# Recommendation tower, one core: three 128-sample embedding tiles in a ring, four products taken one chunk ahead, and a new order of the pass

## What is computed

```python
e = jnp.stack([tbl_0[ids[:, 0]], ..., tbl_25[ids[:, 25]]], axis=1)   # 2048 x 26 x 128
sd = jnp.einsum('bfd,bd->bf', e, dense)
ss = jnp.einsum('bfd,bgd->bfg', e, e)
pairs = ss[:, iu, ju]                                                 # i < j
h = jnp.concatenate([dense, sd, pairs, dense], axis=1)
h = jnp.maximum(h @ W_top1 + b_top1, 0.0)                             # 512
h = jnp.maximum(h @ W_top2 + b_top2, 0.0)                             # 256
y = h @ W_top3                                                        # 1
```

## Time and profile before

| | us |
|---|---|
| median of 3 runs (401.68 to 403.55) | 402.63 |
| the profiled execution | 404.94 |
| its span, first to last instruction | 403.1 |
| PE busy | 337.3 (84%) |
| POOL busy | 277.5 (69%) |
| DVE busy | 234.1 (58%) |
| ACT busy | 204.8 (51%) |
| mean granted TensorE clock | 0.949 |

### The profile page before, as it was taken

One profiled execution on the slowest core, in us unless ns is written; L12 is line 12 of the kernel. 1 busy time (PEld: TensorE's weight loads), 2 busy tenths in 40 slices (PEclk: granted clock), 3 DMA queues, 4 the chain that ended last, 5 costly groups with the idle time before them and its releaser, 6 DMA issues.

```text
span 403.1 us, 14210 instructions
## 1 busy us (share of the span) xinstructions
PE 337.3 (84%) x6216; PEld 301.7 (75%) x6216; DVE 234.1 (58%) x702; ACT 204.8 (51%) x289; POOL 277.5 (69%) x295
## 2 busy tenths in 40 slices
PE   0556889898989889897989899896998989898585
PEld 0545679797878769795979779683987979796384
DVE  0969968682776438680867457670587538640321
ACT  2372545566466534666465553754346654565132
POOL 6777777777777777777777777777777777773000
PEclk9998989999999989999998999998899999899559
DMA  6998233222323214223323325122141323111000
GB/s 166 246 260 261 77 84 96 79 76 83 98 81 78 76 54 110 68 80 81 96 80 79 81 57 121 55 81 78 55 122 54 99 62 81 55 52 36 3 2 1
DMA packets 19118, 35.33 MB, mean 88 GB/s; under 512 B 7168, under 2 KB 8712, under 8 KB 19056
## 3 DMA queue, kind: packets, MB, share of 16 engines
q0 software_dynamic: 9216, 18.89, 17.8%
q1 hardware_dynamic: 9824, 15.52, 13.9%
q10 hardware_dynamic: 16, 0.01, 0.0%
HBM read 34.39 MB, written 0.01 MB: 85 GB/s over the span
## 4 chain that ended last, share of the span: by engine, by line
PE 55%; POOL 12%; ACT 11%; DMA 9%; issue 8%; DVE 3%; SPq 1%; POOLq 0%
PE et_ps L565 23%; POOL rows L290 12%; PE m_ps L525 10%; PE g_ps L486 8%; ACT et L371 8%; PE m_ps L536 6%; PE et_ps L555 5%; DMA et<-tbl_in 5%; DMA rows<-tbl_in,idx 3%; ACT zt_hi L346 2%; PE m_ps L545 2%; DMA idb<-ids_one_hot 1%; DVE one_hot L406 1%; DVE zt_lo L449 1%; DVE z L442 1%
## 5 line engine op out<-in xcount | busy, mean ns | idle before, releaser
L290 POOL DMA_INDIRECT rows<-tbl_in,idx x288 | 276.7, 961 | 89.3 <-issue 84.8
L406 DVE TENSOR_SCALAR one_hot<-idb,first_row 125x256 fp32r<-125x256 int32 x512 | 159.6, 384 | 81.5 <-PE et_ps L565 78.5
L371 ACT COPY et<-et_ps 128x384 f32<-128x384 f32 (+1 forms) x128 | 123.4, 1031 | 97.8 <-PE et_ps L565 76.7
L565 PE MATMUL et_ps<-one_hot,table_hi 125*128 125x256 f32 x512 | 132.7, 297 | 22.2 <-DVE one_hot L406 18.8
L565 PE MATMUL et_ps<-one_hot,table_lo 125*128 125x256 f32 x512 | 127.1, 286 | 0.0
L565 PEld LDWEIGHTS et_ps<-one_hot,table_hi 125*128 125x128 f32 x512 | 100.1, 195 | 29.2 <-issue 20.4
L565 PEld LDWEIGHTS et_ps<-one_hot,table_lo 125*128 125x128 f32 x512 | 100.0, 195 | 0.0
L555 PE MATMUL et_ps<-ident,rows 128*128 128x128 f32 x288 | 51.1, 291 | 16.6 <-DMA rows<-tbl_in,idx 11.9
L486 PE MATMUL g_ps<-et 128*27 128x26 f32 x4096 | 54.0, 193 | 11.4 <-issue 9.2
L486 PEld LDWEIGHTS g_ps<-et 128*27 128x27 f32 x4096 | 45.3, 106 | 23.0 <-issue 15.9
L555 PEld LDWEIGHTS et_ps<-ident,rows 128*128 128x128 f32 x288 | 32.6, 145 | 22.3 <-issue 13.1
(11 more groups left out here) (46 smaller groups left out, 284.5 us busy)
## 6 DMA issues: line engine op xcount, KB each, us to landing
idb<-ids_one_hot SPq DMA_DIRECT2D x32, 256.0 KB
rows<-tbl_in,idx POOLq DMA_INDIRECT x288
et<-tbl_in SPq DMA_DIRECT2D x7, 448.0 KB
xt<-dense_t SPq DMA_DIRECT2D x8, 128.0 KB, 3.9
z<-w_z SPq DMA_DIRECT2D x2, 256.0 KB, 5.9
et<-w SPq DMA_DIRECT2D x1, 512.0 KB, 6.9
gram<-tbl_in SPq DMA_DIRECT2D x1, 448.0 KB
et<-tbl_in SPq DMA_DIRECT2D x7, 52.0 KB
```

What stands on the lines that cost most here:

```text
L290: nc.gpsimd.indirect_dma_start(out=rows[:, r, n, :], out_offset=None, in_=tables[GATHERED[k]], in_offset=bass.IndirectOffsetOnAxis(idx[par ...
L371: nc.scalar.copy(dst, src).then_inc(et_copied, 1)
L406: last = nc.vector.tensor_scalar(one_hot[n % 2][0:KP, k, :], idb[0:KP, n // 2 % ID_RING, n % 2, :], first_row[0:KP, 0:1], float(k), ALU.su ...
L565: last = nc.tensor.matmul(ps[:, n % 2 * CH:n % 2 * CH + CH], part[0:KP, n, k, :], one_hot[n % 2][0:KP, k, :], start=k == 0 and part is tab ...
```

## The change

- `et` becomes one ring of three tiles of 128 samples (two a chunk) where there were two of 256.
- O0 to O3 of chunk c+1 are done at the end of the pass in which the rest of chunk c is looked up; `PLAN` lists all steps of the kernel with their chunk. What waits for what is worked out from the place in this list.
- The one-hot rows are a ring of 16 rows (two units); each row is announced and given back by itself, where a whole unit was. B steps are gone: unit n+1 is built at step O n.
- The order of a pass is another (`PHASE`). G steps come in twos. In passes without a next chunk the steps of that chunk are left out.
- An O pair is copied to `et` in two instructions of 256 columns, one per tile, and the dense features in two of 128.
- At the start the tables go through four places (three in the third tile of `et`, one in `gram`). The dense features and three blocks of the first layer's weights are loaded behind the fourth table. The gather indices are loaded at once for all chunks (the first chunk's 36 columns first).
- As before: eight one-hot tables, 18 gathered ones, a ring of eight slots of rows, 288 gathers, and the same matmuls.

```diff
-SCHEDULE = [(step[0], int(step[1:])) for step in (
-    "O0 B2 G4 O1 B3 G5 T0 G6 O2 B4 G7 O3 B5 A0 T1 A1 O4 O5 A2 T2 A3 T3 Z0 Z1 T4 T5 Z2 B6 B7 L0 T6 L1 T7 "
-    "O6 O7 T8 L2 G0 T9 G1 G2 T10 G3 T11 L3").split()]
+PHASE = [(step[0], int(step[1:])) for step in (
+    "T0 G4 G5 O4 T1 O5 G6 G7 T2 A0 A1 T3 O6 A2 A3 O7 Z0 T4 Z1 T5 Z2 "
+    "T6 G0 G1 L0 T7 G2 G3 T8 L1 O0 T9 O1 L2 T10 O2 T11 L3 O3").split()]
+def later(kind, n):
+    if kind == "O" and n < AHEAD:
+        return 1
+    return -1 if kind in "AZL" or kind == "G" and n >= G_STEPS // 2 else 0
+AHEAD = 4
+OH_RING = 16
+STAGES = 4
+PLAN = [(kind, p + later(kind, n), n) for p in range(-1, NCH + 1) for kind, n in PHASE
+        if 0 <= p + later(kind, n) < NCH]
...
-        one_hot = [sb(f"one_hot{i}", [128, KT, CH], f32r) for i in range(2)]
+        one_hot = sb("one_hot", [128, OH_RING, CH], f32r)
-        et = [sb(f"et{i}", [128, CH * FW]) for i in range(2)]
+        et = sb("et", [128, ET_TILES * TILE_W])
...
+            for n, f in enumerate(ONE_HOT):
+                if n >= STAGES:
+                    sp.wait_ge(table_lo_done, n - STAGES + 1)
+                if n == 6:
+                    load_ids(2)
...
+                if n == 1:
+                    sp.dma_start(idx[:, first:], ids_gather[:, first:]).then_inc(idx_in[1], 16)
+                    load_ids(1)
+                if n == STAGES - 1:
+                    load_dense(0)
+                    load_dense(1)
+                    for k in range(KZ):
...
+                if kind == "O" and n % 2 == 1:
+                    act.wait_ge(oh_used, (c * NO + n + 1) * KT)
+                    src = et_ps[SLOT["O", c, n - 1] % 2][:, :].rearrange("d (f t b) -> d t f b", f=2, t=TILES)
+                    for t in range(TILES):
+                        last = nc.scalar.copy(et_fields(TILES * c + t, NG + n - 1, 2), src[:, t])
+                    last.then_inc(et_copied, 1)
+                if kind == "O" and c == 0 and n + STAGES < NO:
+                    table_hi_part(n + STAGES)
...
+            def build(unit):
+                pair, half = divmod(unit, 2)
+                if half == 0:
+                    dve.wait_ge(idb_in[pair % ID_RING], (pair // ID_RING + 1) * 16)
+                for k in range(KT):
+                    at = unit * KT + k
+                    wait(dve, oh_used, at - OH_RING + 1)
+                    nc.vector.tensor_scalar(one_hot[0:KP, at % OH_RING, :], idb[0:KP, pair % ID_RING, half, :],
+                                            first_row[0:KP, 0:1], float(k), ALU.subtract, ALU.is_equal)\
+                        .then_inc(oh_ready, 1)
+                if unit + 1 < NO:
+                    table_lo_part(unit + 1)
...
+                if kind == "G" and c == 0 and n == G_STEPS // 2 - 1:
+                    split_weights()
...
+                    for k in range(KT):
+                        at = (c * NO + n) * KT + k
+                        pe.wait_ge(oh_ready, at + 1)
...
+                        last.then_inc(oh_used, 1)
```

556 lines of the change are left out of this document (253 added, 303 removed).

## The result

| | before | after |
|---|---|---|
| median (lowest to highest of 4 runs each) | 403.09 (401.68 to 404.51) | 422.64 (418.79 to 424.97) |
| profiled execution; its span | 404.94; 403.1 | 420.60; 418.8 |
| last gather starts | 366.57 | 380.28 |
| from there to the end of the span | 36.5 | 38.5 |

The account below looks back on a forecast made before the run. GpSimd's unhindered chain of 288 gathers was taken to bound the kernel: 3.33 + 363.24 + (36.53 + 0.3) + 1.84 = 405.2 us profiled, 402.9 beside the median of 402.63; range 399.8 to 406.8.

Parts of the forecast that it names:

- The pass: One TensorE pass over a chunk: claimed to keep its pace of about 43 us, covered by the gathers, price 0.
- The walk: Step-by-step sum of TensorE's work through one pass, ending at 41.8 us; with hand-overs 43, bounds 41.5 and 46.
- About 1 us for hand-overs: Allowance in a TensorE pass for hand-overs between engines, added to the walk to reach 43 us.
- The 43.2 of before: TensorE's pass in the kernel before, measured between 79.92 and 123.08, when held by its own work and its partners.
- The start: Loading of tables and first gathers: claimed TensorE frees row slots about 1.1 us early, cost nothing, bounds 0 and +4.
- Rival 2: GpSimd is held up in the start by late tables; at 4 us late, 405.9 us; chance 0.14.
- Rival 3: TensorE's pass exceeds 45.2 us, so it falls behind its rows; at 46 us a pass, 408.8 us; chance 0.12.
- the lag: How far T0 of the second chunk runs behind its rows: claimed 8 us, as before, worked off by the last T11.
- 8.7 us for the missing steps: Last pass, T0 to T11: time off a full pass, for three O fewer and L3 and O3 standing behind T11.
- The point of 45.2: TensorE pass length in us up to which gathers cover it; from there on the cover is gone.
- The end: After the last gather: terms 0.8 + 1.0 - 1.5 sum to +0.3 us, bounds -3.3 and +1.8.
- term (d): End of kernel: TensorE's 0.32 and 2.73 us issue gaps in the last products shrink; -1.5 us, bounds 0 and -3.05.

Follow-up runs that it names:

- order of before, new rings: Changed kernel keeping its rings, row-wise hand-over, copies per tile and load start, but with the kernel before's whole order, builds included, and no products ahead: 404.43 us.
- own builds: Combined kernel with O7's unit built right behind O6's, the next chunk's first two behind Z2, and A0, O6, A1, T3, A2, O7, A3, T4 in sequence: 405.53 us.
- old steps, builds at O: Changed kernel with the kernel before's order of steps and no products ahead, but VectorE still building unit n+1 at step O n: 427.31 us.
- T0 late: Changed kernel with G4 and G5 moved ahead of T0 in the pass: 420.2 us, ratio 1.0396.
- spacer: Changed kernel with one small VectorE instruction, adding an SBUF column to itself, behind each packing of z: 424.99 us, ratio 1.0528.
- indices early: Changed kernel with the fourth pair of indices loaded ahead of SyncE's waits for the last weights: 421.24 us, ratio 1.0465.
- builds alone: Changed kernel with only VectorE's builds moved: O7's unit right behind O6's, the next chunk's first two behind the split of Z2: 410.06 us, ratio 1.0106.
- combined: Changed kernel with three edits: O6 ahead of A0 and next chunk's first build behind Z2; G4, G5 ahead of T0; fourth index pair early: 410.11 us.
- builds away from packing: Changed kernel with O6 ahead of A0 on all engines and the next chunk's first unit built behind the split of Z2: 424.71 us, ratio 1.0559.
- by units of eight: Changed kernel with one-hot rows handed over by whole units of eight again, ring and order kept: 444.26 us, ratio 1.0925.
- one gather of three: Both kernels with only the first of three tables in a slot gathered: changed kernel 410.8 us, kernel before 389.05 and 395.15 us.

## Where the prediction went wrong, step by step

**The frame held.** The time is the later of GpSimd's chain with a tail of about 36 us and TensorE's own chain. The kernels above, by that rule:

| kernel | last gather | tail | held gathers | set by |
|---|---|---|---|---|
| before | 366.57 | 36.5 | 0 | gathers |
| order of before, new rings | 367.50 | 36.1 | 0 | gathers |
| own builds | 368.39 | 36.4 | 0 | gathers |
| old steps, builds at O | 392.89 | 36.0 | 7, of 4.5 to 5.0 us | gathers |
| T0 late | 381.87 | 36.1 | 9 | gathers |
| spacer | 387.50 | 35.1 | 12 | gathers |
| changed | 380.28 | 38.5 | 8 | TensorE, by 2 to 3 us |
| indices early | 380.18 | 38.1 | 6 | TensorE, by 2 us |
| builds alone | 366.46 | 41.3 | 0 | TensorE |
| combined | 367.12 | 42.8 | 0 | TensorE |
| builds away from packing | 367.86 | 52.5 | 0 | TensorE |
| by units of eight | 393.10 | 53.2 | 9 | TensorE |

**The pass was the step that failed.** The walk gave 41.8 us and 1 us of hand-overs; T0 to T0 took 46.4 in the pass from 211.33 to 257.74. Its pieces, each against the walk: T0's wait for the copy of O2/O3 was missing (+1.3). The G pairs were taken at 1.5 to 1.6 from runs of 64 that followed one another; they take 1.8 to 2.1 (four pairs, +1.3). The first layer's L0, at 3.8 us instead of 2.9, ran its first matmuls slowly (0.41 us each, not 0.28) behind the waits of Z:

```profile
230.46 0.43 PE L482 MATMUL a_ps<-ident,z 64*128 64x64 f32 x4 [1.11 <-issue]
230.82 0.55 PE L435 MATMUL et_ps<-ident,rows 128*128 128x128 f32 x3
231.29 2.04 PE L462 MATMUL g_ps<-et 128*27 128x26 f32 x128
...
233.64 0.41 PE L498 MATMUL m_ps<-x_hi,w_lo 128*128 128x256 f32 x1
```

Two windows of this L0 (columns as for the passes; the granted clock is the third figure from the end) show the lower of the two levels, 1.2 GHz, and then the higher:

```profile
233.20:234.80 1.60, 1.60 (x12) 1.55 (x9) 0.00 (x0) 0.88 (x1) 1.29 (x2) 0.50 0.32 79
235.20:236.80 1.60, 1.60 (x16) 1.60 (x15) 0.00 (x0) 0.00 (x0) 1.14 (x2) 1.00 0.14 41
```

I had put the lower clock into the end of the kernel only, not into the pass (+0.9 here; in the pass from 175.91 on, at 1.00, L0 takes 3.06). O1, at 3.4 instead of 3.0, started behind a build that had itself waited for the split of L1 (+0.4). The other pieces add 0.7. The walk had seen the waits for builds and packing, each within about 0.6 us. What it lacked was T0's wait for the copy, the price of the G products and the clock behind a wait. "About 1 us for hand-overs", which had to hold all that the walk left out, was the mis-sized term; it was 4.6.

**The same error hid the width.** The bounds of 41.5 and 46 came from the walk, and the measured mean of 46.9 lies above them. The 43.2 of before was taken as a check of the walk, though it holds the hand-overs of another order, and is one pass at full clock.

**The start was late, and I priced it at nothing.** T0 of the second chunk was placed right behind 61.6 and ran at 69.45. The rows before it came nearly as walked: 37.2 for T1 and 40.8 for T2 (forecast 36.9 and 40.6), and GpSimd was never held (its longest wait for TensorE is 0.3 us). The fourth pair of indices was the wait that I had not followed: it stands behind SyncE's two waits for tables, and cost VectorE 6.2 us. The chain that leads to this T0 runs through it and through VectorE's builds and splits to 63.50, and only then through TensorE (pieces of the chain):

```profile
37.98 5.28 DMA idb<-ids_one_hot
...
59.29 4.21 DVE one_hot L366 x14
...
68.23 1.18 ACT et L291 x2
```

The build of O1 began at 59.22 where I had 53, which is 6.2 of the 8 us; the copy of O2/O3 ahead of T0, which the walk lacked here too, is 1.3 more. Loading the indices early moved T0 by only 1.0 all the same: then the chain lies on TensorE and the copies of its pairs from 35 us on, and that path, too, is 7 us longer than I had it. Two paths were late, and either alone would have been enough. Rival 2, GpSimd held up at the start, didn't happen.

**Rival 3's mechanism is what happened; its sum was not right.** It said: the lag behind the rows at T0 of the second chunk, and six times what the pass has over 45.6, less what the last pass gives back, since it has no products of a next chunk. The measured lag is 69.45 - 54.1 = 15.3, and it grows by 6 x (46.9 - 45.6) = 7.8. With rival 3's 8.7 us for the missing steps the last pass would give back 3.6 and T11 be 19.5 us late. But from its T0 (351.00) to T11 (386.81) the last pass took 35.8 us, 11.1 less than an average one, and gave back 6.0: 17.1 late, where T11 ran 17.5 later than before (369.31). From T11 to the end it was 32.0 us instead of 33.8. That is 15.7, the difference of the two spans (418.8 and 403.1). The sum with 8.7 comes to 402.9 + 19.5 = 422.4, beside the measured 422.6, but by luck: the profiled executions, from which its marks come, lie only 15.7 us apart, the medians 19.6. For the kernel with the builds alone the same steps give 14.8 - 3.1 - 6.0 = 5.7 for T11 (measured 5.9) and 4.6 for the span (4.6); with the builds away from the packing 14.6 + 9.4 - 5.8 = 18.2 (18.4), and 17.3 (17.3).

So the mechanism was right, and three of its terms were not: the lag, taken as 8 and measured as 15.3; the pass, priced at 46 with a chance of 0.12 because the walk gave 43; and the last pass. The point of 45.2 belongs to a lag of 8. With 15.3, and 6.0 given back, TensorE is late from a pass of about 44 us on.

**What the forecast had no term for.** That a build of VectorE can hold a gather for as long as it lasts. The excess of 4.5 us over 1.25 a step was called one "without a recorded cause", and I took GpSimd's chain as one that nothing on the chip holds up. It is held up: by 13.5 us in the changed kernel, 26 us with the old steps. That cost nothing more here because TensorE was later still. With TensorE on time it would have been enough: 13.5 us on the last gather are, by the frame, a time near 416 (an estimate), outside the range as well.

**The end** was forecast at +0.3 and came to -1.8 behind T11 (33.8 to 32.0). T10 and T11 ran together at full clock, since TensorE was behind its rows, so L3 took its old 1.02 us. The gap in the last 256 G products shrank from 2.73 to 1.90:

```profile
386.48 0.82 PE L435 MATMUL et_ps<-ident,rows 128*128 128x128 f32 x6
387.57 1.02 PE L518 MATMUL m_ps<-h,w3s 128*1 128x256 f32 x4 [0.27 <-ACT h L330]
389.12 1.42 PE L462 MATMUL g_ps<-et 128*27 128x26 f32 x146 [0.53 <-ACT et L307]
392.44 1.52 PE L462 MATMUL g_ps<-et 128*27 128x26 f32 x110 [1.90 <-issue]
```

The two gaps of before (0.32 and 2.73) come to 1.15 us more than the one of now, where term (d) took 1.5. But that one gap is 1.97 to 2.69 us in the eight other kernels with all gathers and this order of the end, so no run shows that the order shortened it. It, too, goes with a packet of q8, 390.15 to 391.08, as the 2.73 of before does (372.96 to 374.40).

No version was faster than the kernel before. The best two are level with it, as the frame says: 288 gathers of 1.25 us and a tail of 36 us are a floor that none of these orders lowered.

## What to carry to other kernels

When an engine with 84% busy time follows another one's pace with 2.4 us a pass to spare at most, that spare is what an edit of the order can lose, and it has to be priced by what each new wait drags behind it (a slower clock, a bank's copy), not by the length of the wait. With two limits a few us apart, single edits show nothing: here three that gave +2, -2 and -1 us alone gave -12.5 together, so a null result for one edit can mean that the other limit still stands. When an order is moved back for a test, all queues have to be moved back: the old steps with builds at new places were 23 us slower than the old steps with the old places, and put the loss on the wrong part.

## What the runs showed of the hardware

- A gather can be held until a build has ended, 2.3 to 2.9 us for one beside eight rows and 4.5 to 5.0 beside sixteen, against 0.94. Behind a packing of `z` (a small addition between them or not) the held ones start from 0.38 us ahead of the first row to 0.45 behind it. Those that start ahead of it, or within 0.01 us behind it, end 0.12 us behind the last row; those that start 0.09 us or more behind it end 0.82 behind. With one gather of three, held ones start 2.9 to 3.3 us into builds of sixteen rows behind splits, and end 0.8 to 1.4 us behind them. Yet with all gathers, builds behind a split left a gather that starts 0.09 us ahead of them (kernel before, build at 257.90) or 0.08 us behind their start (changed kernel, 255.53) at 0.94. What makes the difference is open.
- A build that holds a gather runs at the pace of one that has no gather beside it: 2.18 us for eight rows (2.18 to 2.19 with one gather of three), where 2.3 to 2.7 is usual beside gathers.
- In this order, hand-over by rows instead of by units of eight is worth over 16 us, and its waits cost nothing that could be measured (order of before: 404.4 with it, 404.9 without).
- With the same instructions, passes of the changed kernel at mean granted clocks of 1.00 took 45.49 and 46.85 us, at 0.96 46.36 to 46.88, at 0.90 49.26: one short stretch at the lower clock can't be told from the other differences of two passes.
- TensorE stands for 1.5 to 3.5 us in runs of the small G products, in all fourteen traces; each of the 27 gaps of that length goes with a 16 KB packet of the instruction queue q8 that ended 1.2 to 1.6 us before the gap did.
